# Attention pass of a graph network: a group's one-hots in one VectorE instruction, two groups ahead, and transposes through one PSUM bank

## What is computed

```python
h = (x @ W).reshape(N, H, C)                    # H = 4 heads of 64
e = leaky_relu(a_src[src] + a_dst[dst], 0.2)
p = exp(e - m[dst])                             # the kernel takes an upper bound for m
alpha = p / segment_sum(p, dst)[dst]
out = segment_sum(alpha[:, :, None] * h[src], dst).reshape(N, H * C) + bias
```

## Time and profile before

| | |
|---|---|
| median of 3 runs | 9568.67 us |
| the profiled execution: its own time, its span | 9618.35 us, 9616.5 us |
| mean granted TensorE clock | 0.732 |
| busy share PE, DVE, ACT, POOL | 61%, 43%, 16%, 59% |
| attention pass, first one-hot to last | 211.1 to 3095.2 us of the span |

### The profile page before, as it was taken

One profiled execution on the slowest core, in us unless ns is written; L12 is line 12 of the kernel. 1 busy time (PEld: TensorE's weight loads), 2 busy tenths in 40 slices (PEclk: granted clock), 3 DMA queues, 4 the chain that ended last, 5 costly groups with the idle time before them and its releaser, 6 DMA issues. The chain is left out here.

```text
span 9616.5 us, 116917 instructions
## 1 busy us (share of the span) xinstructions
PE 5882.3 (61%) x27644; PEld 4830.0 (50%) x27645; DVE 4091.1 (43%) x11540; ACT 1580.0 (16%) x3782; POOL 5636.3 (59%) x6057
## 2 busy tenths in 40 slices
PE   3667776666655268886144444444444469999894
PEld 2555655544544257775133222322222358888884
DVE  4555666666656520001444444444443422222225
ACT  0111121111111023322000000000000123333331
POOL 3665666666554556665566666666666346666662
PEclk7777777777777579998566666666666758888876
DMA  3332332222222234444332222222221012222335
GB/s 108 82 84 79 82 84 78 76 75 76 71 67 70 76 106 134 137 135 123 106 88 85 81 79 80 82 79 81 80 79 52 21 43 65 63 64 67 66 62 159
DMA packets 428348, 799.55 MB, mean 83 GB/s; under 512 B 129927, under 2 KB 267899, under 8 KB 427982
## 3 DMA queue, kind: packets, MB, share of 16 engines
q0 software_dynamic: 237808, 481.17, 20.2%
q1 hardware_dynamic: 190430, 317.21, 9.8%
HBM read 726.97 MB, written 70.98 MB: 83 GB/s over the span
## 5 line engine op out<-in xcount | busy, mean ns | idle before, releaser
L979 PE MATMUL g_pM<-g_G,g_S 128*128 128x260 f32 (+1 forms) x6656 | 2451.1, 521 | 1683.9 <-issue 666.8
L979 PEld LDWEIGHTS g_pM<-g_G,g_S 128*128 128x128 f32 x6656 | 1599.0, 259 | 2355.1 <-issue 1153.0
L728 POOL DMA_INDIRECT g_G<-table,g_STG x1664 | 1653.2, 994 | 1172.9 <-issue 493.0
L741 POOL DMA_INDIRECT g_G<-table,g_IDX x1664 | 1583.2, 951 | 917.5 <-issue 474.9
L833 DVE TENSOR_TENSOR acc<-g_pM,acc 128x260 f32 (+1 forms) x3328 | 1412.0, 424 | 1369.7 <-remote 634.9
L1543 POOL DMA_INDIRECT q_G<-table,slot x1072 | 1041.8, 972 | 636.3 <-issue 288.3
L601 POOL DMA_INDIRECT slots<-sort_PAIR,sort_ADDR x1024 | 1025.2, 1001 | 519.8 <-issue 310.9
L824 DVE TENSOR_SCALAR g_S<-iota,g_REL,g_WT 128x128 f32<-128x128 f32 x1664 | 597.8, 360 | 466.4 <-issue 278.3
L966 PE MATMUL g_pA<-keep,g_ST 128*128 x3328 | 517.4, 281 | 418.8 <-ACT g_ST L911 298.1
L966 PEld LDWEIGHTS g_pA<-keep,g_ST 128*128 128x128 f32 x3328 | 501.7, 233 | 455.7 <-issue 452.8
L955 PE MATMUL g_pT<-ident,g_S 128*128 128x128 f32 x1664 | 326.9, 331 | 517.2 <-DVE g_S L822 487.6
(11 more groups left out here) (318 smaller groups left out, 6385.4 us busy)
## 6 DMA issues: line engine op xcount, KB each, us to landing
e_W<-in_L_ffn_W SPq DMA_DIRECT2D x210, 512.0 KB
sort_PAIR<-slot_rows SPq DMA_DIRECT2D x66, 512.0 KB
g_G<-table,g_STG POOLq DMA_INDIRECT x1664
g_G<-table,g_IDX POOLq DMA_INDIRECT x1664
ys_all<-ew_Y SPq DMA_DIRECT2D x196, 128.0 KB
sm_Y<-ys_all SPq DMA_DIRECT2D x28, 896.0 KB, 10.5
q_ST<-slot_rows SPq DMA_DIRECT2D x34, 512.0 KB
sort_ADDR<-slot_rows SPq DMA_DIRECT2D x34, 512.0 KB
```

The source lines that it names most:

```text
L728: pool.indirect_dma_start(G[:, r, u, :], None, table, bass.IndirectOffsetOnAxis(ap=STG[:, r, u:u + 1].bitcast(U32), axis=0)).then_inc(gath ...
L741: pool.indirect_dma_start(G[:, r, u, :], None, table, bass.IndirectOffsetOnAxis(ap=IDX[:, k * GRP + u:k * GRP + u + 1].bitcast(U32), axis= ...
L979: pe.matmul(pM[u % BANKS][:, 0:width], S[:, r, u, :], G[:, r, u, :], start=True, stop=True).then_inc(s["sum"], 1)
```

## The change

One VectorE instruction, `onehots`, builds all 8 one-hots of a group. It compares a copy of the column numbers in PSUM (`pN`, written once) with the group's 8 columns of `REL`, both broadcast. It is called in step k for group k + 2. The first addition moves ahead of `ARG`, the scan of the rank rounds moves from before `L` to after the one-hots. The buffer `pT` shrinks from two PSUM banks to one, so that each half's transposes wait for the copy of the half before; `spread` of group k + 1 waits for both `Z` of group k.

```diff
-            pT = sc.ps(f"{tag}_pT", [P, GRP, P])
+            pT = sc.ps(f"{tag}_pT", [P, HG, P])
+            pN = sc.ps(f"{tag}_pN", [P, P])
...
+            def onehots(rnd, r):
+
+                k = rnd * RINGS + r
+                at_least(v, s["sum"], (k - RINGS + 1) * GRP)
+                v.tensor_tensor(S[:, r], pN[:, :].unsqueeze(1).broadcast_to([P, GRP, P]),
+                                REL[:, bass.ds(k * GRP, GRP)].unsqueeze(2).broadcast_to([P, GRP, P]),
+                                ALU.is_equal).then_inc(s["onehot"], 1)
...
-                next_onehots((0, 1))
-                if phase == "rank" and r % 2 == 1:
-                    scan_block(b, r // 2)
-
                 v.wait_ge(s["z"], k * 2 + 2)
...
-                next_onehots((2, 3))
+                add_before(0)
                 v.wait_ge(s["lr"], k + 1)
                 v.tensor_tensor(ARG[:, par], L[:, par, 0], L[:, par, 1], ALU.subtract).then_inc(s["arg"], 1)
-                for u in range(HG):
+                if exists(*after(rnd, r, 2)):
+                    onehots(*after(rnd, r, 2))
+                if phase == "rank" and r % 2 == 1:
+                    scan_block(b, r // 2)
+                for u in range(1, HG):
                     add_before(u)
-                    next_onehots((HG + u,))
...
-                    a.activation(ST[:, sl, :], pT[:, sl, :], ACT.Copy).then_inc(s["copied"], 1)
+                    a.activation(ST[:, sl, :], pT[:, :, :], ACT.Copy).then_inc(s["copied"], 1)
...
-                at_least(pe, s["copied"], 2 * k - 1 + hf)
-                pe.wait_ge(s["onehot"], k * GRP + (hf + 1) * HG)
+                at_least(pe, s["copied"], 2 * k + hf)
+                pe.wait_ge(s["onehot"], k + 1)
...
-                at_least(pe, s["z"], 2 * k - 2)
+                at_least(pe, s["z"], 2 * k)
```

More of the change, by code:

```diff
@@ L621, in graph_pass @@
     if attend:
-        names += ["turned", "copied", "ad", "z", "lr", "arg", "p", "pcol", "gp"]
+        names += ["iota", "turned", "copied", "ad", "z", "lr", "arg", "p", "pcol", "gp"]
     if ranking:
@@ L820, in onehot @@
                     at_least(v, s["sum"], (rnd * RINGS + r - RINGS + 1) * GRP)
[L821 to L825, removed]
+                v.tensor_scalar(S[:, r, u, :], sh.iota[:, :], rel, WT[:, bass.ds(j, 1)],
+                                ALU.is_equal, ALU.mult).then_inc(s["onehot"], 1)
             def add(k, u, blk):
@@ L833, in add, with after, exists @@
                 v.tensor_tensor(sums, pM[u % BANKS][:, 0:width], sums, ALU.add).then_inc(s["added"], 1)
-            def after(rnd, r):
-                return rnd + (r + 1) // RINGS, (r + 1) % RINGS
+            def after(rnd, r, n=1):
+                return rnd + (r + n) // RINGS, (r + n) % RINGS
+            def exists(rnd, r):
+                return not isinstance(rnd, int) or rnd < RND
             def step_attend(rnd, r, phase=None, b=None):
@@ L845, in step_attend @@
                     blk = load_registers(v, regs, BLK, (k - 1) * GRP)
[L847 to L850, removed]
                 def add_before(u):
@@ L891, in step_weighted @@
                     add(rnd * RINGS + r, u, blk[u])
-            for u in range(GRP):
-                onehot(0, 0, u)
             if attend:
+                v.tensor_copy(pN[:, :], sh.iota[:, :]).then_inc(s["iota"], 1)
+                v.wait_ge(s["iota"], 1)
+                onehots(0, 0)
+                onehots(0, 1)
                 over_groups_sorting(v, step_attend, bases, addresses)
@@ L900, in _ @@
             else:
+                for u in range(GRP):
+                    onehot(0, 0, u)
                 over_groups(v, step_weighted)
@@ L951, in transposes @@
             def transposes(k, r, hf):
-                at_least(pe, s["copied"], 2 * k - 1 + hf)
-                pe.wait_ge(s["onehot"], k * GRP + (hf + 1) * HG)
+                at_least(pe, s["copied"], 2 * k + hf)
+                pe.wait_ge(s["onehot"], k + 1)
                 for u in range(hf * HG, (hf + 1) * HG):
-                    m = pe.transpose(pT[:, u, :], S[:, r, u, :], sh.ident[:, :])
+                    m = pe.transpose(pT[:, u - hf * HG, :], S[:, r, u, :], sh.ident[:, :])
                 m.then_inc(s["turned"], 1)
```

## The result

The changed kernel takes **9737.13 us** (median of 4 runs, 9712.12 to 9754.98) against 9568.03 us of the kernel before in the same comparison (4 runs): ratio **1.0159, 95% interval 1.0124 to 1.0194**. It is 1.6% slower. The forecast was 9328, the range ended at 9650; the result is the third rival's, priced at 9743. The profiled execution took 9723.24 us (span 9721.1 us).

What follows compares the result with a forecast made beforehand. No busy engine but a ring of four with late TensorE signals was taken to bound the attention pass; 57 us (first part) plus 184 (second) made 241 less than 9618, 9377, or 9328 against the median; range 9150 to 9650.

Steps and rivals of the forecast that it cites:

- third rival: Attention pass: earlier sums remove GpSimd's pauses, counting rounds fall into bursts of two groups; 9743 up to 10,100 us; slower: 0.17.
- The signals of TensorE still set the pauses. I take the period of the undisturbed rows, 12.4 us: Counting rounds: all 100 groups at 12.4 us instead of 12.97, 57 us less.
- Second part: 54 pairs x (2 x 0.94 + 1.5): Rank rounds: each pair of groups 3.4 us shorter, leaving 26 us; 184 us less.
- The mean of all pairs there is 2 x 14.71 = 29.4 us: Rank rounds: mean time of two groups, from 14.71 us per group; the shown pair takes 32.85 us.
- 174 us: Counting rounds: loss at the second part's 14.71 us per group, 1.74 x 100.
- One-hots: VectorE, attention pass: 208 comparisons of 1.213 us replace 448.3 us, 196 us less, 0.94 us per group.
- lower value of 0.71: VectorE: us saved per group if old one-hots cost 0.24 us each, as back to back (147 us); 0.94 was taken.
- TensorE's wait for one-hots: Attention pass: waits of 53.2 us in the first part and 413.9 in the second forecast to go.
- 1.5 us per pair: Rank rounds: part of 3.5 us gained per pair because transposes no longer wait for same-step one-hots.
- One bank and the later wait for `Z`: TensorE, attention pass: one transpose bank covered by sums of tiles 4 to 7, `spread` behind `Z` free; no cost.
- Scan: VectorE's step: moving scan and first addition costs nothing; bad-side bound 0.4 us per group (83 us).
- GpSimd becomes the bound: Rival, attention pass: late signals thin out, groups follow at 10.4 us, 724 us less, 8845 us; chance 0.12.

Runs made afterwards that it cites:

- p1: Changed kernel plus a 1.7 us GpSimd pause (row-number copy written 256 times) before each group's gathers, late chip: 9343.30 us, 0.9750 of the kernel before.
- e6: Changed kernel with one of two predicated copies moved from the second step's end to the third step, late chip: 9533.34 us, 0.9930 of the kernel before.
- e9: Changed kernel with every predicated copy moved one step on, behind the next step's one-hots, late chip: 9522.54 us, 0.9934 of the kernel before.
- q1: Changed kernel with a shorter GpSimd pause (row-number copy written 128 times) before each group's gathers, late chip: 9360.27 us, 0.9981 of the kernel before.
- q3: Changed kernel with the 1.7 us pause, scan constant from PSUM and one predicated copy of two moved a step on, late chip: 9122.92 us, 0.9727.
- before again: The kernel before, unchanged, run again on a prompt chip: 7916.04 us, ratio 1.0001.
- after again: The changed kernel, unchanged, run again on a prompt chip: 7837.05 us, 0.9902 of the kernel before.
- e4: Changed kernel with column numbers read from SBUF again and transposes over two PSUM banks, prompt chip: 7879.89 us, 0.9947 of the kernel before.

## Why the prediction was wrong, point by point

- **"The signals of TensorE still set the pauses. I take the period of the undisturbed rows, 12.4 us": failed in size.** 12.95 us stayed 13.05 in the counting rounds; the 57 us didn't come.
- **"Second part: 54 pairs x (2 x 0.94 + 1.5)": this step failed.** It let every us saved on VectorE and in TensorE's wait shorten the pair to 26 us. In the locked pattern it takes 32.2 (median of the pairs of neighbours). From 14.66 to 15.87 us the 107 intervals give 129 us more, where 184 less were forecast. I had read correctly that signals come late while bursts follow without a pause, and then subtracted VectorE time from a period that VectorE does not set. What does set it is when TensorE's signals arrive: in p1, with 1.7 us more work but a pause, the same engines do 12.77.
- **"The mean of all pairs there is 2 x 14.71 = 29.4 us":** I took this as one period to shorten, though it was a mixture of two patterns (28 long steps of 107). What matters is how often each occurs; the change took it to 48.
- **The third rival was right in mechanism and in time** (9743 for 9737), and wrong in place: the pauses of the counting rounds survived, and the rank rounds, which already had the pairs, took them up for good. Its 174 us were for the counting rounds, which lost 9; the rank rounds lost 110. So the agreement in time is luck.
- **One-hots: right on the instruction** (1217 ns for 1213; 195 us less), too high on the engine. VectorE's busy time fell by 107 us in the two parts, 0.51 per group, below my lower value of 0.71 from pairs back to back: small instructions overlap their neighbours more than that (before, VectorE's instructions in the pass add up to 341 us more than its busy time, after to 196).
- **TensorE's wait for one-hots: gone as forecast** (487.6 to 11.5 us), worth nothing on prompt chips, where GpSimd's idle time stayed at 478.2 us; on late ones no run has it alone. The 1.5 us per pair that I gave it were an error.
- **One bank and the later wait for `Z`: nothing, right** (0.9998 and 1.0006). **Scan: "nothing, with 0.4 us on the bad side": wrong in both directions.** On prompt chips its place is nearly the whole gain, through what it does to GpSimd's instructions; on late ones it gives 1.1% alone and, with the one-hots, the loss.
- **"GpSimd becomes the bound"** is what holds on prompt chips, at 10.1 us for my 10.4. The trace of one late chip could not show it.

**What stays open:** why signals come late on some chips; why some pass in the middle of a burst in e6, e9 and q1; by what rule the order of VectorE's work locks the pairs; and whether one version wins on both kinds. e6 and e9 beat both kernels on late chips (0.993) and were not run on prompt ones. The best there, q3 (0.9727), has a pause that cost 3.8% on a prompt chip.

## What to carry to other kernels

When an idle gap ends with a signal that is recorded as given long before, the gap belongs to no engine's work, and time saved on an engine must not be subtracted from it: in the first comparison 107 us less on VectorE shortened nothing. Look at which pattern the steps fall into, and count the patterns rather than take their mean; a forced pause of an idle-looking engine is a cheap test. And a VectorE instruction beside GpSimd's gathers costs them time by where its operands lie: one input from PSUM freed them here, at no price in its own duration.

## What the runs showed of the hardware that I had not expected

- TensorE's finished signals can reach the other engines late while indirect DMAs are issued without a pause, on some chips: a `Z` 13.8 us after its spread's recorded end, a copy 10 us after its transposes'. On a prompt chip (before again) no copy of groups 100 to 199 is over 0.04 us late. A pause of 1.9 us in every group lets most of them through, one of 1.05 us only in part. The same kernel takes 7910 us on one chip and 9585 on another.
- A gather of 0.95 us takes up to 3.01 us beside a scan of two SBUF inputs (after again) and up to 2.01 beside such a comparison (e4), and the 0.2 us copy of row numbers 1.05 beside a predicated copy. With one input of the scan or the comparison in PSUM their part of it is gone.
- More work can be faster: with 1.7 us more per group on GpSimd the change stands at 0.9750 of the kernel before, without it at 1.0159.
